# A last stage of attention and a mixture of experts: sixteen expert tiles per chunk in place of eighteen

## The reference, cut to what matters

```python
pw = _partition_weights()                      # 11 x 6, rows that sum to 1
token_repr = x.mean(axis=1)
probs = jax.nn.softmax(token_repr @ router_w.T, axis=-1)
topk_vals, topk_idx = jax.lax.top_k(probs, 2)
topk_vals = topk_vals / topk_vals.sum(axis=-1, keepdims=True)
expert_weights = jnp.einsum('bk,bke->be', topk_vals, pw[topk_idx])
h = gelu(jnp.einsum('bsd,edf->ebsf', x, W1) + b1[:, None, None, :])       # 6 experts, f = 341
out_e = jnp.einsum('ebsf,efd->ebsd', h, W2) + b2[:, None, None, :]
return jnp.einsum('be,ebsd->bsd', expert_weights, out_e)
```

## Time and profile before

| | |
|---|---|
| median of three runs | 859.66 us |
| the profiled execution's own time | 855.88 us |
| its span, first to last instruction | 854.0 us |
| mean granted TensorE clock | 0.849 of full speed |
| TensorE matmul busy | 612.0 us (72%) |
| VectorE busy | 630.7 us (74%) |
| ScalarE busy | 518.1 us (61%) |
| GpSimd busy | 327.8 us (38%) |

### The profile page before, as it was taken

One profiled execution on the slowest core, in us unless ns is written; L12 is line 12 of the kernel. 1 busy time (PEld: TensorE's weight loads), 2 busy tenths in 40 slices (PEclk: granted clock), 3 DMA queues, 4 the chain that ended last, 5 costly groups with the idle time before them and its releaser, 6 DMA issues.

```text
span 854.0 us, 10965 instructions
## 1 busy us (share of the span) xinstructions
PE 612.0 (72%) x3096; PEld 471.3 (55%) x3097; DVE 630.7 (74%) x1351; ACT 518.1 (61%) x781; POOL 327.8 (38%) x345
## 2 busy tenths in 40 slices
PE   6994752652717356299683699266999999999997
PEld 4552752652717346275453599233666666766655
DVE  1785597999999999997885122268888988887752
ACT  1587999998999898972233234244566465464432
POOL 0463110213414132250477144314555556554432
PEclk9995776877869686789876699667999999999999
DMA  5380035344445553433312366100000000000000
GB/s 175 117 304 17 0 66 89 75 80 83 84 76 104 100 98 71 71 71 103 120 32 72 100 187 185 59 28 0 2 1 10 1 10 9 1 10 10 2 10 18
DMA packets 26273, 56.50 MB, mean 66 GB/s; under 512 B 4007, under 2 KB 15376, under 8 KB 26005
## 3 DMA queue, kind: packets, MB, share of 16 engines
q0 software_dynamic: 5728, 24.56, 15.3%
q1 hardware_dynamic: 19924, 30.88, 11.7%
q10 hardware_dynamic: 576, 0.52, 0.2%
HBM read 29.89 MB, written 10.17 MB: 47 GB/s over the span
## 4 chain that ended last, share of the span: by engine, by line
PE 50%; DVE 14%; ACT 13%; issue 11%; POOL 6%; DMA 3%; POOLq 1%; SPq 0%; ACTq 0%; DVEq 0%
PE psum L1944 10%; PE psum L1681 3%; PE psum L1745 3%; PE psum L1746 3%; PE psum L1747 3%; PE psum L1874 3%; PE psum L1882 3%; PE psum L1974 2%; PE psum L1936 2%; DVE s_R L1608 2%; ACT s_R L863 2%; DVE s_R L1193 2%; PE psum L263 2%; ACT s_R L873 2%; PE psum L1938 2%
## 5 line engine op out<-in xcount | busy, mean ns | idle before, releaser
L1745 PE MATMUL psum<-s_xn_lo,s_split_hi 128*128 128x368 f32 x256 | 95.1, 372 | 139.1 <-ACT s_R L893 134.4
L1745 PEld LDWEIGHTS psum<-s_xn_lo,s_split_hi 128*128 128x128 f32 x256 | 54.9, 215 | 143.8 <-ACT s_R L893 137.1
L1944 PE MATMUL psum<-s_R 128*128 128x368 f32 (+1 forms) x288 | 101.2, 477 | 4.1 <-ACT s_R L1017 4.1
L1212 DVE TENSOR_TENSOR_SCAN s_R<-s_R 128x2944 f32<-128x2944 f32 x16 | 100.7, 6292 | 0.8
L1746 PE MATMUL psum<-s_xn_hi,s_split_lo 128*128 128x368 f32 x256 | 92.2, 360 | 0.0
L1747 PE MATMUL psum<-s_xn_hi,s_split_hi 128*128 128x368 f32 x256 | 91.7, 358 | 0.0
L1017 ACT ACTIVATE s_R<-psum,s_cols 128x368 f32<-128x368 f32 x96 | 50.6, 567 | 51.8 <-PE psum L1938 51.8
L724 POOL TENSOR_TENSOR s_R<-s_R 128x368 f32<-128x368 f32 x47 | 45.0, 956 | 73.4 <-DVE s_R L1487 53.5
L754 POOL TENSOR_TENSOR s_R<-s_R 128x368 f32<-128x368 f32 x48 | 46.7, 973 | 57.0 <-DVE s_R L1608 55.4
L1944 PEld LDWEIGHTS psum<-s_R 128*128 128x128 f32 (+1 forms) x288 | 51.2, 189 | 28.6 <-issue 8.2
L900 ACT ACTIVATE s_R<-psum,s_cols 128x736 f32<-128x736 f32 x64 | 55.8, 877 | 14.6 <-PE psum L1747 9.7
(11 more groups left out here) (244 smaller groups left out, 1607.7 us busy)
## 6 DMA issues: line engine op xcount, KB each, us to landing
s_xnfm<-s_R POOLq DMA_DIRECT2D x14, 1472.0 KB, 10.5
s_R<-in_w SPq DMA_DIRECT2D x28, 256.0 KB
s_R<-in_xg SPq DMA_DIRECT2D x7, 744.0 KB, 4.2
x_sorted<-in_x_init SPq DMA_DIRECT2D x1, 5082.0 KB
s_wBC<-in_wBC SPq DMA_DIRECT2D x8, 256.0 KB, 2.6
s_R<-x_sorted SPq DMA_DIRECT2D x28, 66.0 KB
s_R<-in_w SPq DMA_DIRECT2D x1, 1536.0 KB, 6.5
s_R<-y_rows SPq DMA_DIRECT2D x8, 184.0 KB
```

Of the source, the lines that this page charges most:

```text
L1212: dve.tensor_tensor_scan(bufB[:, u], ra[:, u], bufB[:, u], 0.0, ALU.mult, ALU.add).then_inc(ra_free, 1)
L1745: pe.matmul(bank(c), w_hi[:, s, u, k, :], xn_lo[:, a:b], start=True, stop=False)
L1944: ins = pe.matmul(bank((2, 4)[e % 2]), w, fh[0:kk, e % 3, j], start=(j == 0), stop=(j == FT - 1))
```

## The change

The third tiles of the six experts (85 units each, 510 together) are packed into four mixed tiles of 128 (`NR` = 4), so a chunk has 16 tiles. A mixed tile holds units of several experts, so its hidden values are multiplied by their expert's weight before the second layer: `weigh_rest`, one VectorE instruction over 128 x 1472 numbers, both inputs in SBUF. Its weights `wr` come from a mask (`rmask`) and `ew` in `expert_weights`. The four mixed tiles' second layer adds up in one bank as a seventh unit, which ScalarE copies to `ftmp` (`rest_out`). The bias b2 is added in `weigh_expert`, now a scalar_tensor_tensor; `bb` is gone. GpSimd's sum begins with the shares of units 0 and 1, so it has six additions per chunk as before. The slices of `FFN` move on all engines, and TensorE gets three products into bank 3 ahead of `shares_fm` in rounds 2 to 7 (`fill_pause(3)`), whose result nothing reads. The loads keep their number (8 in that group) and almost their size.

```diff
@@ constants and layout
-    FT = 3
-    FR = FF - 2 * D
+    FT = 2
+    NR = -(-NE * (FF - FT * D) // D)
+    NU = NE + 1
+    NT1 = NE * FT + NR
@@ order of the steps
         FFN = ([(1, e, j) for e in (0, 1, 2) for j in range(FT)]
                + [(2, e, j) for e in (0, 1) for j in range(FT)]
-               + [(1, e, j) for e in (3, 4) for j in range(FT)] + [(2, e, j) for e in (2, 3) for j in range(FT)]
-               + [(1, 5, 0), (1, 5, 1)] + [(2, 4, j) for j in range(FT)] + [(1, 5, 2)]
-               + [(2, 5, j) for j in range(FT)])
+               + [(1, 3, 0), (1, 3, 1)] + [(1, NE, r) for r in range(NR)]
+               + [(1, 4, 0), (1, 4, 1)] + [(2, e, j) for e in (2, 3) for j in range(FT)]
+               + [(1, 5, 0), (1, 5, 1)] + [(2, e, j) for e in (4, 5) for j in range(FT)]
+               + [(2, NE, r) for r in range(NR)])
+        def added(g):
+            return g // NU * NE + max(g % NU, 1)
@@ GpSimd
-                other = bb.rearrange("p (j o) -> p j o", o=1).to_broadcast([D, CB, L]) if e == 0 else a3
-                pool.tensor_tensor(a3, t3, other, ALU.add).then_inc(facc_add, 1)
+                g = f * NU + e
+                if e == 1:
+                    unit_out(pool, f, 0)
+                    if f:
+                        pool.wait_ge(fT_ready, f)
+                unit_out(pool, f, e)
...
+                pool.tensor_tensor(facc, ftmp[:, g % 2], ftmp[:, 1 - g % 2] if e == 1 else facc, ALU.add)\
+                    .then_inc(facc_add, 1)
@@ ScalarE
+            def rest_out(f):
...
+                act.wait_ge(fo_mm, g + 1)
+                act.wait_ge(facc_add, added(g - 2))
+                act.activation(ftmp[:, g % 2], bank((2, 4)[g % 2]), ACT.Copy).then_inc(fr_out, 1)
-                gelus(c - 1, 0, 9)
+                if c >= NCH:
+                    rest_out(c - 2)
+                gelus(c - 1, 0, 6)
+                if c < NCH:
+                    rest_out(c - 2)
+                gelus(c - 1, 6, 12)
@@ VectorE
+                dve.scalar_tensor_tensor(ftmp[:, g % 2].rearrange("p (j l) -> p j l", j=CB),
+                                         bank((2, 4)[g % 2]).rearrange("p (j l) -> p j l", j=CB),
+                                         b2T[:, e:e + 1], w, ALU.add, ALU.mult).then_inc(fo_free, 1)
+            def weigh_rest(f):
...
+                dve.wait_ge(f_free, 2 + tile_no1(f, NE, NR - 1) + 1)
+                r3 = fr.rearrange("p r (j l) -> p (r j) l", j=CB)
+                w = wr.rearrange("p r (j o) -> p (r j) o", o=1).to_broadcast([D, NR * CB, L])
+                dve.tensor_tensor(r3, r3, w, ALU.mult).then_inc(fr_weighed, 1)
...
                     expert_weights(f - 1)
+                    if not att:
+                        weigh_rest(f - 1)
...
+                weigh_expert(f - 1, 4)
                 if tail:
                     split_stream(f)
...
-                        weigh_expert(f - 1, 4)
+                        weigh_expert(f - 1, 5)
+                        if att:
+                            weigh_rest(f - 1)
...
-                    if o == 5 and tail:
+                    if o == 4 and tail:
                         router_weights(f)
@@ TensorE
+            def fill_pause(n):
+                for _ in range(n):
+                    pe.matmul(bank(3), w_proj, w_qkv.rearrange("p k d -> p (k d)")[:, 0:CT], start=True, stop=True)
...
-                ffn(f - 1, 18, 20)
+                ffn(f - 1, 16, 18)
                 if tail:
                     project(f)
-                ffn(f - 1, 20, 21)
+                ffn(f - 1, 18, 19)
                 result_tm(c - 3)
-                ffn(f - 1, 21, 22)
+                ffn(f - 1, 19, 20)
                 if att:
                     scores(c)
-                ffn(f - 1, 22, 24)
+                ffn(f - 1, 20, 22)
                 if att:
                     scores_tm(c)
-                ffn(f - 1, 24, 33)
+                ffn(f - 1, 22, 26)
                 if att:
+                    if c >= 2:
+                        fill_pause(3)
                     shares_fm(c)
-                ffn(f - 1, 33, 35)
                 if tail:
                     norm_transposes(pe, nF, f % 2, f, (5, 5))
+                ffn(f - 1, 26, 28)
...
-                    if o == 0:
-                        ffn(f - 1, 35, NF)
-                    else:
+                    if not att:
+                        if o == 0:
+                            ffn(f - 1, 28, NF)
+                        else:
+                            ffn(f, 2 * o - 2, 2 * o)
+                    elif 1 <= o <= 3:
                         ffn(f, 2 * o - 2, 2 * o)
+                    elif o == 4:
+                        ffn(f - 1, 28, 30)
+                    elif o == 5:
+                        ffn(f - 1, 30, NF)
+                        ffn(f, 6, 8)
+                    elif o == 6:
+                        ffn(f, 8, 12)
...
-                ffn(f, 12, 15)
+                ffn(f, 12, 14)
                 if tail:
                     router_spread(f)
-                ffn(f, 15, 18)
+                ffn(f, 14, 16)
```

More of the change, by code:

```diff
@@ L428, in audio_tower @@
         posc = take(CT, parts=K)
-        v1 = take(NE, FF)
-        v2 = take(NE, 2, D)
-        v2b = take(NE, D, parts=FR)
-        b1b = take(NE, parts=FR)
+        v1 = take(NT1, D)
+        v2 = take(NT1, D)
+        b1r = take(NR)
+        rmask = take(NR, NE)
         b2T = take(NE)
@@ L461, in audio_tower @@
         fh = take(3, FT, CT)
+        fr = take(NR, CT)
+        wr = take(NR, CB)
+        wrt = take(NR, CB, NE)
         facc = take(CT)
@@ L475, in audio_tower @@
         ew = take(NE, CB)
-        ewb = take(NE, CB)
-        bb = take(CB)
         assert taken[0] <= W_AT
@@ L494, in audio_tower, with tile_no1, unit_out @@
                + [(2, e, j) for e in (0, 1) for j in range(FT)]
-               + [(1, e, j) for e in (3, 4) for j in range(FT)] + [(2, e, j) for e in (2, 3) for j in range(FT)]
-               + [(1, 5, 0), (1, 5, 1)] + [(2, 4, j) for j in range(FT)] + [(1, 5, 2)]
-               + [(2, 5, j) for j in range(FT)])
+               + [(1, 3, 0), (1, 3, 1)] + [(1, NE, r) for r in range(NR)]
+               + [(1, 4, 0), (1, 4, 1)] + [(2, e, j) for e in (2, 3) for j in range(FT)]
+               + [(1, 5, 0), (1, 5, 1)] + [(2, e, j) for e in (4, 5) for j in range(FT)]
+               + [(2, NE, r) for r in range(NR)])
+        ORDER1 = [(e, j) for layer, e, j in FFN if layer == 1]
+        def tile_no1(f, e, j):
+            return f * NT1 + ORDER1.index((e, j))
+        def added(g):
+            return g // NU * NE + max(g % NU, 1)
+        def unit_out(eng, f, e):
+            if e == NE:
+                eng.wait_ge(fr_out, f + 1)
+            else:
+                eng.wait_ge(fo_free, f * NE + e + 1)
         NF = len(FFN)
@@ L547, in _ @@
                 sp.dma_start(dst, t[name]).then_inc(wE_ready, 16)
-            for dst, name in ((v1, "v1"), (v2, "v2"), (v2b, "v2b"), (b1b, "b1b"), (b2T, "b2T"), (pwT, "pwT"),
+            for dst, name in ((v1, "v1"), (v2, "v2"), (b1r, "b1r"), (rmask, "rmask"), (b2T, "b2T"), (pwT, "pwT"),
                               (diag, "diag"), (ones4, "ones4")):
@@ L716, in add_expert @@
                     return
[L717 to L724 removed]
+                g = f * NU + e
[4 more added lines that the diff above has]
+                unit_out(pool, f, e)
+                if e > 1:
+                    pool.wait_ge(facc_add, added(g - 1))
+                pool.tensor_tensor(facc, ftmp[:, g % 2], ftmp[:, 1 - g % 2] if e == 1 else facc, ALU.add)\
+                    .then_inc(facc_add, 1)
             def rstd_e(c):
@@ L1050, in _ @@
                     act.activation(v1_hi[:, :, :], v1, ACT.Copy).then_inc(v1_hi_ready, 1)
-                gelus(c - 2, 18, 21)
+                gelus(c - 2, 16, 18)
                 if c < NCH:
@@ L1054, in _ @@
                     exponential(c)
-                gelus(c - 2, 27, 33)
+                gelus(c - 2, 22, 24)
                 if c < NCH:
@@ L1652, in _ @@
                     if o == 3:
-                        weigh_expert(f - 1, 5)
                         if tail:
                             router_second(f)
-                    if o == 5 and tail:
+                    if o == 4 and tail:
                         router_weights(f)
```

118 lines of the change are left out of this document (70 added, 48 removed).

## The result

| | before | after |
|---|---|---|
| median of the runs | 859.38 us (4 runs, 855.71 to 859.77) | 869.87 us (4 runs, 869.26 to 870.55) |
| ratio, after to before | | 1.0133, 95% interval 1.0119 to 1.0146 |
| profiled execution, its span | 855.88 us, 854.0 us | 870.55 us, 868.7 us |
| start of round 1 in the span | 579.1 | 582.1 |
| VectorE's copy of the weights, one to the next, rounds 2 to 6 | 32.51, then 32.95 to 32.97 | 34.93 to 35.97 |

The change makes the kernel 1.3% slower. From the start of round 1 the profiled executions differ by 286.7 - 274.9 = 11.8 us; the 3 us ahead of it lie in stages that the change leaves alone. By the distances between those copies, rounds 2 to 6 lose 12.1 (176.4 - 164.4), round 7 loses 1.5, round 1 gains 0.3. In the tail 4.9 should have come back, and 1.4 did.

What follows compares the result with a forecast made beforehand. TensorE was taken as full, with VectorE and ScalarE just beside it in a ring through three engines. Rounds 2 to 6 +2.0, round 7 +0.1, rounds 8 and 9 -4.9: -2.8, so 857 us, range 851 to 863.

Steps and rivals of the forecast that it cites:

- that ring closes at the same length: From VectorE's weights copy to the score products: 8.1 us of work, ending near 7.0 at worst, so no length added.
- the shares can't be there before 14.2: Ahead of the shares' transposes: scores end at 7.5, plus 6.7 us over ScalarE and VectorE; transposes move from 14.3 to 14.2.
- slack just named: VectorE ahead of the score products, half a product ahead of TensorE's need; was to hold 0.2 us of grown weights' product and sum.
- Shares to first offset: Stream's transposes moved ahead of expert 5 behind the shares: first offset at 17.45 in place of 18.4, 0.9 us earlier.
- weigh_rest: Between offset 0 and offset 1, on the ring: 1.6 us; GpSimd taken to wait beside it, zero on VectorE.
- The mixed products: TensorE behind the third offset: 8.9 us to the router's product's end, next round at 33.4 against 33.0, plus 0.4 per round.
- Two tiles fewer: TensorE, 2.25 us less per chunk, 18.0 for eight; the 2.25 saved ahead of the shares are lost in a pause.
- The fill: Three float32 products, 1.9 us in six rounds, ahead of the shares' transposes: costs nothing under the pause.
- The tail: Rounds 8 and 9, without attention, where TensorE comes last nearly throughout: -3.4 and -1.5, together -4.9 us.
- A: Rival, slower: offset 0 to offset 2 grows beyond weigh_rest through GpSimd's additions, 1.0 to 1.6 us a round; 862; chance 0.18.
- D: Rival: TensorE's clock falls in the pauses, up to 3 us in each of six rounds; at half, 866; chance 0.08.
- B: Rival: collisions of GpSimd's additions with the router's steps fall away, rounds 0.3 to 0.4 shorter; 853; chance 0.17.

Runs made afterwards that it cites:

- e13: Changed kernel with four fillers; GpSimd's bias addition waits for the weights, its addition of unit 4 for the stream's split; 865.17 us, ratio 1.0057.
- e5: Kernel before plus one VectorE product of 1472 numbers, in place on unread score products behind expert 4's weighing; 867.60 us, ratio 1.0114.
- e9: Changed kernel with the mixed tiles' weighing cut to one number per partition and five fillers in place of three; 854.32 us, ratio 0.9967.
- e6: Kernel before with the third tiles of experts 4 and 5 cut to 8 of 368 columns in both layers; 851.30 us, ratio 0.9925.
- e2: Changed kernel with four filler products in place of three ahead of the shares' transposes; 866.79 us, ratio 1.0106.
- e1: Changed kernel without the three filler products ahead of the shares' transposes; 875.71 us, ratio 1.0199.
- e10: Changed kernel with four fillers and the weighing of unit 4 put back behind offset 0; 878.93 us, ratio 1.0262.
- e16: Changed kernel with four fillers, the two GpSimd waits (bias, unit 4), and GpSimd weighing two of four mixed tiles at the round's head; 869.34 us, ratio 1.0111.
- e11: Changed kernel with four fillers and the mixed tiles weighed by GpSimd in four products in rounds with attention; 870.39 us, ratio 1.0153.
- e15: Changed kernel with four fillers, two GpSimd waits (bias, unit 4), earlier router's product in attention rounds, and GpSimd weighing two mixed tiles; 860.43 us, ratio 1.0007.

## Why the prediction was wrong

The forecast was 857 us within 851 to 863, and the chances stood at 0.53 for faster. The kernel is slower by 1.3%, outside the range.

**The step that failed** is in the part on the mixed products, where VectorE's work to the score products "would end near 7.0 at worst, half a product ahead of TensorE's need. So that ring closes at the same length". The product itself ended at 7.1, as worked out. But I had compared it with TensorE's scores only, and not followed what VectorE and GpSimd have behind it. In the earlier trace rows the exponential shows no wait, because ScalarE was busy normalizing until just then; the subtraction ahead of it also ended just then, as a row of before that I had not laid beside it shows:

```profile
686.14 0.54 DVE L1487 TENSOR_TENSOR s_R<-psum,s_R 128x368 f32<-128x368 f32 x1 [0.45 <-PE psum L1944]
...
687.24 0.92 DVE L1535 TENSOR_TENSOR s_R<-psum,s_R 92x448 f32<-92x448 f32 x1
```

687.24 + 0.92 = 688.16, and the exponential starts at 688.19. The weighing of unit 2 ahead of it had waited for TensorE and started 11.1 behind the copy; in after it waits for GpSimd and starts 10.95 behind it (694.03 - 683.08). Several chains were level there within some 0.3 us, and with the copy 1.0 nearer to the round's start the one through VectorE and GpSimd became the last: the shares' transposes start 15.0 behind the start of q, k, v in place of 14.2. That is 0.9 of the 1.6 us a round that the forecast missed. The same step stood under the bound "the shares can't be there before 14.2", which was taken as the time when they are there. Round 7, without that chain, shrank in this piece as forecast. The "slack just named", in which the grown weights' product was put, wasn't there either: e13 prices its collision at 0.5 a round.

**Shares to first offset.** The order behind them was right (transposes, expert 5, spread; -0.69 in place of -0.9). The missing 0.2 is the split at 1.12 us beside GpSimd's addition: with the split at 0.54, in e13, the piece is 4.17, so -1.0.

**weigh_rest** took 1.68 where I took 1.6, and e5 and e9 confirm that it counts with its whole length, 1.8 between the first and the third offset. GpSimd waited for it (its addition took 2.34), so zero on VectorE was right in this place, and wrong in the places next to it.

**The mixed products** behind the third offset: 9.06 on TensorE in place of 8.9; right. In round 7 this piece was 7.82 before, so the change adds 1.3 there; the forecast of +0.1 for that round missed this.

**Two tiles fewer**: that the 2.25 us are "lost in a pause" was right in the main; e6 gives the rest a size, 0.75 a round.

**The fill** costs nothing on the path, as forecast (e2).

**The tail.** 3.4 + 1.5 were forecast. Without a fall of the clock (e2) round 8 gains 1.5 and what lies behind it 1.4; in the change's own profile a fall in round 8 takes 1.7 of that. The waits came as walked (unit 0 in round 9 1.53 in place of 1.65, the normalization 1.82 in place of 1.8; TensorE idle for 3.5 of round 8 in e2, as summed). What was too small is TensorE's work in round 8: 22.1 us busy in e2, where the sum had 20.2. TensorE in order of time, after, round 8:

```profile
834.67 0.54 PE L265 MATMUL psum<-s_ident,s_xs 92*128 92x92 f32 x4 [1.82 <-DVE s_xs L240]
835.04 5.60 PE L2001 MATMUL psum<-s_R 128*128 128x368 f32 x12
...
854.11 0.89 PE L2001 MATMUL psum<-s_R 128*128 128x368 f32 x2 [1.53 <-DVE s_R L1527]
```

**The rivals.** A had the right side, and its mechanism, a stretch of the offsets that grows beyond weigh_rest, was the smaller part of it: 6.14 against 5.9. D, at 0.08, was true in part, three falls worth about 3 us together (e2). TensorE: Matmul & The Clock Gate (section HAM oscillation) of the Trainium skill warned of waits between bursts; the runs agree in kind. The waits of that section's case are 3 to 5 us long; here the clock fell behind shorter ones, behind pauses of 1.1 and 0.5 us in two of five rounds (after), behind 2.96 or 1.88 us in all six (e1, e10). GPSIMD Engine Reference (section Specifications) of the Trainium skill says that VectorE's instructions with two SBUF inputs, and those in a 2-port performance mode, contend with GpSimd for the shared SBUF interfaces. e16 agrees on the first kind, with 1.5 us. L240, stretched by 1.44 in e11, reads a single tile; whether it runs in the second kind's mode no run here shows. B failed: the collisions moved and did not fall away.

So per round, if the prices add up: weighing +1.75 (e9), the two new collisions +0.77 (e13), two tiles fewer -0.75 (e6), together 1.8 of the measured 2.0. The remaining 0.2 was not tried by itself, and e6 leaves the worth of two whole tiles open.

## What to carry to other kernels

Where several engines form a ring, cut it at a few points and add up what the change does to every piece; work taken off the fullest engine counts only in its own piece, and an instruction put on the ring counts whole. When a step moves nearer to its consumer, follow everything queued behind it on its engine to the next hand-over, and don't take a row without idle time for slack. Filling TensorE's pauses with idle products is cheap insurance for its clock, and worth sizing until no fall is left.

## What the runs showed of the hardware

A pause of TensorE can cost more than its length: with a wait of 1.88 us for an offset, e10 ran at 0.57 of the clock in the 4 us from 707 on. It need not: behind the pause of 1.82 us in round 8 the clock fell in after and not in e2. GpSimd's products stretched VectorE's normalization with one SBUF tile and per-partition scalars (L240) from 1.11 to 2.55 us, while an offset, which reads PSUM, kept its time beside an addition of GpSimd. VectorE and GpSimd in order of time, e11, round 4:

```profile
707.46 0.66 DVE L1670 TENSOR_TENSOR s_R<-psum,s_R 128x344 f32<-128x344 f32 x3
...
707.62 0.99 POOL L743 TENSOR_TENSOR s_R<-s_R 128x368 f32<-128x368 f32 x1 [2.01 <-DVE s_R L1540]
```

GpSimd's operation on 4 numbers took 3.24 us in after and ended when the seven VectorE products beside it had ended. In e15 it started just ahead of them and took 0.23, and they took 3.85 in place of 3.08. GpSimd in order of time, e15, round 4:

```profile
685.50 0.23 POOL L760 TENSOR_SCALAR s_pa<-s_mv 92x4 f32<-92x4 f32 x1
```
